# A feed-forward stage taken tile by tile with its first bias summed in PSUM, and an attention front split into two halves of the tokens

## What is computed

```
x = x + tanh(g_xattn[0]) * L0_xattn(layernorm(x), ctx)
x = x + tanh(g_ffn[0])   * L0_ffn(layernorm(x))      # attention, then 16 experts, top 4
x = x + tanh(g_xattn[1]) * L1_xattn(layernorm(x), ctx)
x = x + tanh(g_ffn[1])   * L1_ffn(layernorm(x))
```

```
def act_quant(x):    scale = 127 / clip(max|x| of the token, 1e-5)
                     return clip(round(x * scale), -128, 127) / scale
def weight_quant(w): scale = 1 / clip(mean|w|, 1e-5)
                     return clip(round(w * scale), -1, 1) / scale
def bitlinear(x, w, b): return act_quant(x) @ weight_quant(w).T + b
h = gelu(bitlinear(x, w1, b1))            # 512 -> 2048
return bitlinear(h, w2, b2)               # 2048 -> 512
```

## Time and profile before

| what | us |
|---|---|
| median of 3 runs | 2841.33 (2840.94 to 2842.41) |
| the profiled execution, its own time | 2844.89 |
| its span | 2843.1 |
| up to the end of the experts' work on DVE | 2128.7 |
| from there to the first softmax work of DVE | 88.0 |
| the second attention proper | 432.0 |
| the feed-forward's weights | 55.0 |
| the feed-forward's 8 tiles, to the end | 139.4 |

### The profile page before, as it was taken

The page is one execution under the profiler, slowest core; times in us unless marked ns, Lnnn a source line. Parts: engine busy times, 40 slices in busy tenths (PEclk is TensorE's granted clock), DMA queues, the critical chain, the costliest instruction groups (busy, mean ns, idle before and its releaser), DMA issues. The chain is left out here.

```text
span 2843.1 us, 46195 instructions
## 1 busy us (share of the span) xinstructions
PE 2385.3 (84%) x14782; PEld 1985.4 (70%) x14790; DVE 1755.0 (62%) x3889; ACT 1482.6 (52%) x3037; POOL 1086.3 (38%) x1545
## 2 busy tenths in 40 slices
PE   5999999999984888998887557999994798898355
PEld 3778788787874788888886446999983576677222
DVE  2555555555544666666664744556655787788486
ACT  3444444444433666666665454444432777778543
POOL 0322222322221444444442366777751644445000
PEclk9999999999996999999998777999997899999688
DMA  3000000000001000000001475677656422321100
GB/s 112 19 12 18 7 18 11 7 18 11 7 1 41 20 19 18 0 18 18 18 18 33 153 251 177 187 198 198 186 127 184 103 69 61 92 78 67 78 8 22
DMA packets 123652, 190.90 MB, mean 67 GB/s; under 512 B 18272, under 2 KB 66656, under 8 KB 121760
## 3 DMA queue, kind: packets, MB, share of 16 engines
q1 hardware_dynamic: 111408, 161.69, 18.9%
q0 software_dynamic: 10992, 25.96, 4.2%
q10 hardware_dynamic: 1152, 2.10, 0.3%
HBM read 143.58 MB, written 46.14 MB: 67 GB/s over the span
## 5 line engine op out<-in xcount | busy, mean ns | idle before, releaser
L435 ACT ACTIVATE x_p<-x_p,x_least 128x1024 f32<-128x1024 f32 x128 | 147.3, 1151 | 307.4 <-DVE x_least L391 307.4
L375 DVE TENSOR_TENSOR x_pT<-pair,x_pT 128x512 fp32r<-128x512 f32 x256 | 164.3, 683 | 122.4 <-ACT x_pT L454 122.4
L469 POOL TENSOR_TENSOR x_carry<-x_rtotal 128x1 f32<-128x1 f32 x128 | 24.7, 193 | 559.9 <-DVE x_rtotal L368 559.9
L2157 PE MATMUL pair<-m_h,e_w 128*128 128x320 f32 x1536 | 230.4, 310 | 1.1 <-DVE m_h L2072 1.1
L2157 PEld LDWEIGHTS pair<-m_h,e_w 128*128 128x128 f32 x1536 | 228.9, 189 | 2.7 <-issue 1.5
L537 PE MATMUL pair<-x_pT,x_v 128*128 128x256 f32 x1536 | 209.6, 293 | 9.2 <-DVE x_pT L375 9.2
L537 PEld LDWEIGHTS pair<-x_pT,x_v 128*128 128x128 f32 x1536 | 193.9, 194 | 26.3 <-issue 18.3
L993 ACT ACTIVATE s_p<-s_p,s_least 128x128 f32<-128x128 f32 (+3 forms) x256 | 143.6, 561 | 123.2 <-DVE s_least L903 123.2
L565 PE MATMUL pair<-x_kT,x_qT 128*128 128x512 f32 x768 | 207.0, 404 | 0.0
L2500 DVE TENSOR_REDUCE z_most<-pair 128x1 f32<-128x1008 f32 x128 | 154.0, 1203 | 72.8 <-PE pair L2610 50.9
L1131 PE MATMUL pair<-s_pT,s_v 128*128 128x256 f32 (+1 forms) x1152 | 158.5, 284 | 47.1 <-DVE s_pT L880 47.1
(11 more groups left out here) (337 smaller groups left out, 6108.5 us busy)
## 6 DMA issues: line engine op xcount, KB each, us to landing
e_raw<-in_L_ffn_w SPq DMA_DIRECT2D x48, 1024.0 KB, 5.8
z_v<-z_vst SPq DMA_DIRECT2D x16, 768.0 KB, 3.6
z_kS<-z_k SPq DMA_DIRECT2D x24, 512.0 KB, 10.3
z_vS<-z_v SPq DMA_DIRECT2D x8, 1536.0 KB, 6.5
f_raw<-in_L_ffn_w SPq DMA_DIRECT2D x2, 4096.0 KB, 13.4
z_qS<-z_q SPq DMA_DIRECT2D x24, 256.0 KB, 4.6
s_wraw<-in_L_ffn_wq SPq DMA_DIRECT2D x9, 512.0 KB, 4.4
x_wq<-in_L_xattn_Wq SPq DMA_DIRECT2D x8, 512.0 KB, 3.7
```

Source lines behind the costliest of these rows:

```text
L375: dve.tensor_tensor(pT[1][:, keys, q * P:(q + 1) * P], TR[j][:, :].rearrange("p (k n) -> p k n", n=P), pT[0][:, keys, q * P:(q + 1) * P].b ...
L435: act.activation(p[n][:, :], p[n][:, :], ACT.Exp, scale=-1.0, bias=least[:, n:n + 1], accum_out=total[:, n:n + 1]).then_inc(s_ex, 1)
L2157: mm = pe.matmul(GU[m % 2][:, j * BANK:j * BANK + CAP], w[x0][:, c, m * P:(m + 1) * P], XS[s][x1][:, c, :], start=(n == 0 and c == 0), sto ...
```

## The change

In the front: the three loads that the query weights need are issued by SP at the end of the experts' program, after a wait for the experts' engines (`s_freed`) and ahead of the wait for the sums; `centre_vector` comes ahead of the adds on DVE; the adds, the statistics, the root and the reciprocal go by halves of 4 tiles; the first root is ACT's first instruction there and the second stands in step 2; the keys and values of the second sequence are loaded after the first 4 tiles' queries; and `z_qstlo` is computed by POOL, two tiles behind its scaling, instead of by DVE.

In the feed-forward: the clamp at L2756 goes, since the scaled numbers lie between -127 and 127; `b1` comes to 2 partitions, is split into a high and a low part, and is multiplied by its scale in one more matmul of 4 rows for each bank, ahead of the other four; the 4 rows' factors `u` are made by two small DVE instructions and turned with the tile; Gelu reads PSUM in two parts of 1024 columns and applies `unscale` itself, so that L2775 goes; the loops go and the 8 tiles are written out one by one; and each tile has a scale column of its own.

```diff
 def query_weights(sp):            # called at the end of both variants of the experts' SP program
     sp.wait_ge(s_freed, 2)
     sp.dma_start(wqraw ...); sp.dma_start(bq ...); sp.dma_start(tbo ...)
 def front_sync(sp):
-    (the three loads) ; keys and values of b = 0, 1
+    load_keys(sp, 0, 0); load_values(sp, 0, 0)
...
                         load_queries(sp, 0, t // QT)
+                        if t < QT:
+                            load_keys(sp, 0, 1)
+                            load_values(sp, 0, 1)
...
+                inner_add(dve, 0)          # 4 adds of y3 onto x3
+                inner_half(dve, 0)         # 4 bn_stats, 4 bn_aggr
+                inner_add(dve, 1)
+                inner_scale(dve, 0)        # waits for the root, reciprocal
                 normal(0)
+                normal(1)
+                inner_half(dve, 1)
                 for s in range(STEPS):
+                    if s + 2 == QT:
+                        inner_scale(dve, 1)
-                    if s + 1 < NT:
+                    if s and s + 1 < NT:
                         normal(s + 1)
...
-                        dve.tensor_tensor(stlo[i][:, :, :], tt[u % 2][:, :, :], sthi[i][:, :, :].bitcast(F32), ...)
...
             def front_scalar_tiles(act):
+                inner_root(act, 0)
                 for s in range(STEPS):
+                    if s == 2:
+                        inner_root(act, 1)
...
             def front_gpsimd(pool):
                 for u in range(NT):
                     (scale tile u)
+                    if u >= 2:
+                        low(u - 2)         # waits for z_qsthi of the tile, subtracts
+                low(NT - 2)
+                low(NT - 1)
                 (8 adds of tbo)
```

The feed-forward's new orders, one iteration t of 8 on each engine:

```diff
+ DVE: norm(0), norm(1), norm(2); then for each t:
+      hidden_scale(t)   # max over z, four small, scale and round
+      norm(t + 3)       # as before without the clamp, plus two small ones for u
+      add_out(t - 1)    # waits for output(t - 1), two instructions
+ ACT: round(0), turned(0), round(1), turned(1), gelu(0), round(2); then for each t:
+      hidden_round(t), gelu(t + 1), norm_turned(t + 2), hidden_turned(t), norm_round(t + 3)
+ PE:  turn(0), hidden(0), turn(1), hidden(1), turn(2); then for each t:
+      hidden_turn(t), hidden(t + 2), output(t), norm_turn(t + 3)
   in hidden, for each bank k:
+    pe.matmul(HID_B[k][:, :], uT[s][:, :], brows[:, cols], start=True, stop=False)
-    mm = pe.matmul(..., start=(c == 0), stop=(c == KC - 1))
+    mm = pe.matmul(..., start=False, stop=(c == KC - 1))
   in gelu, for j in range(2):
-    act.activation(z[s][:, :], z[s][:, :], ACT.Gelu)
+    act.activation(z[s][:, half j], HID2[j][:, :], ACT.Gelu, scale=unscale[:, t:t + 1])
```

More of the change, by code:

```diff
@@ L2805, in turned @@
+                dve.wait_ge(s_b, 48)
+                for t in range(AHEAD):
+                    norm(t)
+                for t in range(NT):
+                    hidden_scale(t)
+                    if t + AHEAD < NT:
+                        norm(t + AHEAD)
+                    if t:
+                        add_out(t - 1)
+                add_out(NT - 1)
             def turned(engine, g):
@@ L2851, in gelu @@
-                def gelu(pair):
-                    for s in range(2):
-                        act.wait_ge(s_z, HB * (2 * pair + s + 2))
-                        act.activation(z[s][:, :], z[s][:, :], ACT.Gelu).then_inc(s_g, 1)
-                norm(0, 0)
-                gelu(0)
-                norm(NORMED["rounded"], NORMED["turns"])
-                def body(i):
-                    rounded, turns = first("rounded", i), first("turns", i)
-                    for s in range(2):
-                        whole(zq[s], z[s], rounded + s)
-                        for k in range(2):
-                            copy(zqT[s][:, k * 8:(k + 1) * 8, :], turns + 2 * s + k, k, 8)
-                    if ahead(i, 1):
-                        gelu(i + 1)
-                    if ahead(i, 2):
-                        norm(rounded + HIDDEN["rounded"], turns + HIDDEN["turns"])
@@ new lines, in gelu, with hidden_round @@
+                def gelu(t):
+                    s = t % 2
+                    for j in range(2):
+                        act.wait_ge(s_m1, 2 * t + j + 1)
+                        act.activation(z[s][:, j * 2 * BANK:(j + 1) * 2 * BANK], HID2[j][:, :], ACT.Gelu,
+                                       scale=unscale[:, t:t + 1]).then_inc(s_g, 1)
+                def hidden_round(t):
+                    s = t % 2
+                    act.wait_ge(s_rz, t + 1)
+                    if t >= 2:
+                        act.wait_ge(s_tz, 2 * (t - 1))
+                    act.activation(zq[s][:, :], z[s][:, :], ACT.Copy, bias=-MAGIC).then_inc(s_qz, 1)
@@ L2940, in bit_ffn @@
+                hidden(0)
+                norm_turn(1)
+                hidden(1)
+                norm_turn(2)
+                for t in range(NT):
+                    hidden_turn(t)
+                    if t + 2 < NT:
+                        hidden(t + 2)
+                    output(t)
+                    if t + AHEAD < NT:
+                        norm_turn(t + AHEAD)
             programs["ACT"].append(sizes)
-            statistics(3, x2_done)
+            statistics(3, x2_done, 1)
             programs["SP"].append(sync)
```

340 lines of the change are left out of this document (175 added, 165 removed).

## The result

The changed kernel takes 2809.20 us in the median of 4 runs (2806.28 to 2813.72), the kernel before beside it 2841.87: a ratio of 0.9883, 95% interval [0.9863, 0.9903], 1.2% faster. I had said 2791.3, between 2781 and 2808, so the time lies 18 us above the forecast and just over the range. The profiled execution took 2806.77, with a span of 2804.9: 38.2 less than before where I had summed 50.0. So 11.8 us are to be found inside the profile. The first experiment shows how far single executions stand apart.

What follows compares the result with a forecast made beforehand. No engine was full in the feed-forward's tiles, so their order bound them; the front had a serial chain of waits. Span 2843.1 - 9.5 - 40.5 = 2793.1, 2794.9 executed, less 3.6: 2791.3 us, range 2781 to 2808.

Steps and rivals of the forecast that it cites:

- The centring: Front: DVE's centring of the query weights hides behind the scatters and the sums' load, so its 6.9 us leave the path.
- The adds of `tbo`: End of the front: POOL's eight adds start 2.8 us later but take 10.0 instead of 11.2, with DVE idle.
- The weights' part: Feed-forward's weights: DVE's subtraction ahead of its copies and ACT's new copy of 1.9 cost nothing, at worst +2.3 us.
- rival 1: Feed-forward tiles: PE's clock keeps falling, one slow group a tile costing 13.6 us in all; 2805 us, chance 0.2.
- Rivals 3 and 4: Feed-forward: 3, a wait closes a ring, tiles do not overlap, 2870 us, chance 0.03; 4, tiles stay at 17 us, 0.02.
- rival 2: Front: low parts and scalings at 1.72 us each and both scatters at 7.1, so it gains 4; 2797 us, chance 0.1.
- the stretch: From the experts to the second softmax: -9.9 + 0.8 - 0.4 = -9.5 us, between -11.5 and -6.
- the price of the bias matmuls: Feed-forward tiles on PE: four bias matmuls at 0.23 us each, 0.9 a tile, bounded by 0 and 0.38 each.
- the ring: Feed-forward tiles: the chain of waits between engines takes 18.8 us for two tiles, 9.4 a tile, against PE's 9.3.
- Iteration 1: Start of the feed-forward's tiles: iteration 1 starts 34 us after norm(0), with 1.7 allowed for a low clock.
- the scatter: Seam after the experts: the new load delays one of the last two scatters by 0.8 us, between 0 and 2.5.
- The step to the median: Whole kernel: the median lies 3.6 us below the profiled execution's own time, 2794.9, giving 2791.3.

Runs made afterwards that it cites:

- The first experiment: The changed kernel run again with no edit, to see how far its time and stretches vary; 2810.29 us, ratio 0.9879 to the kernel before.
- c3: Changed kernel with the low parts of the queries (`z_qstlo`) moved back from POOL to DVE; 2810.75 us, ratio 0.9875 to the kernel before.
- a2: Changed kernel with the bias matmul left out of each bank, so b1 is missing from the result; 2801.01 us, ratio 0.9845 to the kernel before.
- a3: Changed kernel with a tile's four bias matmuls grouped ahead of its sixteen others; 2803.91 us, ratio 0.9857 to the kernel before.
- b4: Changed kernel with bias matmuls in bf16 and 128 rows, 124 of them zero, instead of 4; 2802.28 us, ratio 0.9842 to the kernel before.
- b1: Changed kernel with the query weights' load and centring back at their old places, halves kept; 2820.97 us, ratio 0.9914 to the kernel before.
- b2: Changed kernel with the query weights loaded some 28 us earlier, into the experts' first raw buffer; 2806.37 us, ratio 0.9859 to the kernel before.
- c1: Changed kernel with b1 added by DVE out of PSUM and no bias matmuls, tile order kept; 2810.18 us, ratio 0.9866 to the kernel before.
- a1: The changed kernel run again with no edit; 2810.29 us, ratio 0.9879 to the kernel before.
- c2: Changed kernel with a one-column Gelu ahead of the first tile's rounding, to load ACT's table early; 2813.72 us, ratio 0.9879 to the kernel before.
- d1: Changed kernel with early query weights, `tbo` added within the first turn, 128-row bf16 bias matmuls and early Gelu table; 2791.47 us, ratio 0.9813 to the kernel before.
- b3: Changed kernel with POOL's eight adds of `tbo` moved into the first eight units of the attention's first turn; 2802.63 us, ratio 0.9850 to the kernel before.

## Why the prediction was wrong, point by point

**Right.** The stages, and PE as the bound of the tiles. The centring ended 8 us before the sums landed and left the path. From the first add to the first projection I said 12.9 and it was 12.5. Biases 4.1 apart: 4.08. The adds of `tbo` in 10.0: 9.8, and c3 shows that DVE's low part was what had slowed them. They started 3.4 later where I said 2.8; POOL's low part took 1.26 and not my 1.15. The weights' part gave nothing. DVE's 8.8 a tile is the 8.83 of a2, and PE ran at a granted clock of 1.00 in the middle of the tiles, so rival 1 did not come true there. Rivals 3 and 4 did not either. Of rival 2 a part did: the stretch won 6.1 us, between my 9.5 and its 4, and one scatter took more than the 7.1 that it allowed.

**The step that failed, the price of the bias matmuls.** I priced them at 0.23, from rows of the front of the same type and width, and bounded them by 0.38. Those rows have 128 rows of weights and no neighbours of another number; mine have 4, between groups of 128. In the trace they cost 0.50 each (a2), 0.28 with one change a tile in place of four (a3), and 0.21 once they have 128 rows (b4). My bounds were bounds of the matmul alone, and the cost is that of the changes around it. So PE's tile is 10.25, 0.85 more than the 9.4 that I took for the ring: 3.4 us over four iterations. Iteration 1 started at 36.8 instead of 34, and from iteration 5 to the end it took 25.9 instead of 23.8. Together 8.3 us.

b4 has bias matmuls at about the price that I had given them, and shows where the error lies. Its tiles are 8.0 us shorter than the changed kernel's: 3.1 ahead of iteration 1, 4.0 in the four iterations, 1.0 behind them. Its 95.8 is within 0.3 of my 95.5. That a2 comes as near is luck. Without the matmuls its four iterations take 35.3 and not my 37.7, while its start (35.3) and its end (25.3) are longer than I had them. At the start I had counted one group at the low clock, in the first tile; in every profile a group of the second or third tile ran at it too.

**The term that was too small, the scatter.** I had +0.8 for one scatter, up to 2.5. It was 3.3, and all of it from the loads put beside it (b1, b2). I had read the 48 durations as one kind, with 5.3 in the middle and 7.1 as the worst case. They are of several kinds. In the trace of the kernel before the last six, with no load beside them, and the one of 2093.5, which starts 0.3 after a load of 1 MB of expert weights, land in:

```profile
DMA to landing us min/median/max: 4.6/4.8/5.2
...
DMA to landing us min/median/max: 6.8/6.8/6.8
```

All 14 scatters there that start within 0.5 us of such a load take 6.6 to 7.1. My load starts 0.8 ahead of the scatter, so near 7 was what to expect and not the worst case, some 2 more than with no load. The two loads of 256 KB stand beside it too. With them alone the scatter takes 5.1 (b2); with all three 7.7 to 8.1 in ten profiles, more than the two parts add up to. What makes the rest is not shown.

**The wait I did not see.** DVE's subtraction has two SBUF inputs, and POOL's one-column instruction between two scatters reads SBUF: held for 1.1 us here, and seen in all the profiles with the load at its new place (1.27 to 1.71). The Trainium skill (SBUF — State Buffer, "Who interferes with whom") says that a VectorE instruction with two SBUF inputs contends with a GpSimd instruction that reads SBUF, and the trace agrees. I had weighed that rule for the adds of `tbo`, 60 us later, and not asked it of what I moved. Sums later by 3.3 + 1.1 less 0.5 of smaller terms, 3.9 instead of 0.8: 3.1 of the 11.8. With 8.3 from the tiles, 0.7 by which this run's mark lay later, 0.3 between the first add and the maximum, and -0.6 in the attention, the weights and the last store, the 11.8 are accounted for.

**The step to the median.** It was 6.0 of the 18 us, and nothing in the trace gave it. I had taken 3.6 from one profiled execution of the kernel before; a single execution lies on either side of its median. Without that term the forecast and its range would have lain 3.6 higher, and the measured time just inside.

**What stays open.** The maximum lies at 82.0 to 82.4 in two profiles of an unedited front and at 83.4 to 83.8 in six. Up to 0.7 us of it is in the sums, and 1.0 in the first projection: its 12 matmuls take 4.2 to 4.3 in the two, at a granted clock of 0.65, and 5.2 to 5.3 in the six, at 0.50 or 0.51. Why the clock rose sooner in the two is open. Why the stages ahead of the mark take 5 to 8 us more in some runs is open too.

## What to carry to other kernels

A matmul is priced with its neighbours: between matmuls of 128 rows, one of 4 rows cost more than twice its own time (0.50 against 0.21), and in bf16, filled up with zeros to 128 rows, it cost only the 0.21. A price taken from many durations is taken from those with the same neighbours: the middle of 48 scatters said 5.3, those that started beside a load of 1 MB said 6.8. When work is moved into the shadow of a transfer, ask of each instruction and load in the new place what it shares with the chain it hides behind: the early load was worth 8 to 11 us between the sums and the first projection (b1) and gave back 3 to 4, and issued 28 us sooner it gave back 0.3. An edit that takes work off one engine only pays as far as the next bound, and the start of a pipeline, at a low clock, has a bound of its own: c1 had the longer period on its busiest engine and the shorter stage.

## What the runs showed of the hardware

- Between bf16 matmuls of 128 rows, one of 4 rows holds its own weight load 0.42 us and the next one 0.24. It costs 0.50 in fp32r and 0.43 in bf16, against 0.21 for one of 128 rows.
- An indirect scatter takes 4.5 to 5.5 us with no load beside it, 5.1 with two loads of 256 KB, 6.6 to 7.1 when a load of 1 MB starts with it, and 7.7 to 8.1 with all three.
- A GpSimd instruction of 0.18 us takes up to 1.71 under a VectorE instruction with two SBUF inputs (a1). A VectorE normalisation of 0.54 took 3.00 beside a GpSimd instruction of 4.48 with two SBUF inputs, and ended 0.3 after it (b1, one row).
- The low level of PE's clock at the start of the tiles moves with the gaps and does not go away when one of them is shortened (c2, d1). With the same instructions the granted clock over those 35 us was 0.71 to 0.80, and the first output moved by 1.8 us (b3 against the changed kernel).
